# Graph layer with expert feed-forward: node rows kept as f32, added by VectorE, messages folded as f32

## What is computed

```python
def gnn(x, edge_attr, src, dst, ...):
    msg = relu(x[src] + edge_attr @ W_e + b_e)            # 21,250 x 512
    aggr = segment_sum(msg, dst, num_segments=N)          # 1,250 x 512
    h = (1.0 + eps) * x + aggr
    h = silu(batchnorm(h @ W1 + b1, g1, beta1))           # 1,250 x 1,024
    return silu(batchnorm(h @ W2 + b2, g2, beta2))
x = x + gnn(layernorm(x), ...)
x = x + ffn(layernorm(x), ...)    # each of 16 experts takes its 156 best tokens, gelu, weighted sum
```

## Time and profile before

| | us |
|---|---|
| median of 3 timed runs | 695.65 |
| their least and greatest | 694.82, 698.22 |
| span of the profiled execution | 727.8 |
| start, up to the first gather | 34.2 |
| edge loop, first gather to last fold | 34.2 to 329.1 |
| rest (dense layers, gate, experts) | 329.1 to 727.8 |

### The profile page before, as it was taken

One profiled execution on the slowest core, in us unless ns is written; L12 is line 12 of the kernel. 1 busy time (PEld: TensorE's weight loads), 2 busy tenths in 40 slices (PEclk: granted clock), 3 DMA queues, 4 the chain that ended last, 5 costly groups with the idle time before them and its releaser, 6 DMA issues.

```text
span 727.8 us, 14614 instructions
## 1 busy us (share of the span) xinstructions
PE 538.5 (74%) x5341; PEld 397.1 (55%) x5341; DVE 459.4 (63%) x1110; ACT 366.9 (50%) x630; POOL 358.3 (49%) x257
## 2 busy tenths in 40 slices
PE   2377788789868787798999985711599996888840
PEld 2244455446536454464555544511599986888830
DVE  7544456566746565576648867787679976668610
ACT  3843344445544454464648406630178875568720
POOL 1177777777777777600000000230347856688742
PEclk9998989999999999999999997755589999899985
DMA  7478786867777776804500034541269996643432
GB/s 189 144 192 208 189 205 180 208 179 202 200 190 198 191 198 180 199 19 166 181 1 1 1 115 141 174 158 41 58 202 281 265 268 181 180 101 54 69 40 35
DMA packets 75292, 108.91 MB, mean 150 GB/s; under 512 B 32139, under 2 KB 36803, under 8 KB 75246
## 3 DMA queue, kind: packets, MB, share of 16 engines
q0 software_dynamic: 43712, 53.95, 31.0%
q1 hardware_dynamic: 30364, 53.80, 24.6%
q10 hardware_dynamic: 1170, 0.55, 0.4%
HBM read 95.25 MB, written 12.79 MB: 148 GB/s over the span
## 4 chain that ended last, share of the span: by engine, by line
PE 46%; issue 16%; DMA 11%; DVE 9%; POOL 9%; ACT 6%; DVEq 1%; another core or an unknown queue 1%; ACTq 0%; POOLq 0%; SPq 0%
PE bank L1288 15%; PE bank L1269 9%; DMA out<-rows_z,idx 7%; PE bank L1247 5%; PE bank L1254 5%; POOL out L464 5%; PE bank L1256 4%; PE bank L1304 3%; POOL big L455 2%; PE bank L1230 2%; ACT big L576 2%; POOL big L445 1%; DVE edge_home L927 1%; DMA big<-token_rows,idx 1%; DMA pair<-node_rows,edge_home 1%
## 5 line engine op out<-in xcount | busy, mean ns | idle before, releaser
L918 DVE SCALAR_TENSOR_TENSOR big<-bank,big 125x512 f16<-125x512 f32 x170 | 116.4, 689 | 108.8 <-ACT big L576 63.6
L1288 PE MATMUL bank<-big,pair 128*128 128x156 f16 (+2 forms) x1824 | 173.6, 257 | 5.1 <-DVE big L1153 4.1
L576 ACT ACTIVATE big<-bank 125x512 f16<-125x512 f32 x170 | 98.8, 598 | 125.6 <-PE bank L1269 91.6
L1288 PEld LDWEIGHTS bank<-big,pair 128*128 128x128 f16 x1824 | 143.9, 102 | 30.4 <-DVE big L1153 6.3
L445 POOL DMA_INDIRECT big<-node_rows,edge_home x90 | 109.6, 1218 | 64.4 <-issue 54.2
L445 POOL DMA_INDIRECT pair<-node_rows,edge_home x80 | 98.2, 1227 | 30.0 <-issue 21.3
L464 POOL DMA_INDIRECT out<-rows_z,idx x32 | 85.1, 2658 | 45.4 <-DVE rows_z L1161 19.5
L1247 PEld LDWEIGHTS bank<-edge_home,big 125*128 125x128 f16 x1400 | 68.9, 99 | 55.9 <-issue 24.8
L475 POOL TENSOR_TENSOR big<-aggT,big 125x512 f16<-125x512 f32 x10 | 11.3, 1154 | 166.6 <-ACT big L663 166.6
L1247 PE MATMUL bank<-edge_home,big 125*128 125x64 f16 x1400 | 78.1, 195 | 15.4 <-issue 13.1
L455 POOL DMA_INDIRECT big<-token_rows,idx x32 | 51.1, 1596 | 52.6 <-DVE idx L1142 43.8
(11 more groups left out here) (207 smaller groups left out, 876.4 us busy)
## 6 DMA issues: line engine op xcount, KB each, us to landing
raw<-in_L_ffn_w SPq DMA_DIRECT2D x14, 1024.0 KB
edge_home<-in_L_ffn_w SPq DMA_DIRECT2D x6, 1024.0 KB
xs_home<-in_L_ffn_w SPq DMA_DIRECT2D x6, 1024.0 KB
aggT<-in_L_ffn_w SPq DMA_DIRECT2D x6, 1024.0 KB, 7.2
pair<-in_edge_attr SPq DMA_DIRECT2D x36, 140.0 KB
raw<-in_L_gnn_W SPq DMA_DIRECT2D x16, 256.0 KB
xs_home<-in_x SPq DMA_DIRECT2D x5, 448.0 KB
node_rows<-big SPq DMA_DIRECT2D x5, 448.0 KB
```

The lines of the kernel that those rows point to most:

```text
L576: act.activation(msg[:, b * J + j, 0, :], bank[j][0:P, :], ACT.Relu).then_inc(msg_hi, 1)
L918: dve.scalar_tensor_tensor(out=msg[:, b * J + j, 1, :], in0=bank[j][0:P, :], scalar=0.0, in1=msg[:, b * J + j, 0, :], op0=ALU.max, op1=ALU ...
L1288: last = pe.matmul(bk, weights(i, k), values(j, k), start=(begin and p == k == 0), stop=(end and p == 2 and k == n - 1), skip_group_check= ...
```

## The change

- `node_rows` holds each node as 512 f32 values, the normalised tile as it is; ScalarE's and VectorE's passes for the halves go. A node is still 2,048 B.
- VectorE adds the gathered row, times 8, to the product in bank j (L922 of the changed kernel) and writes the bank; the two row matmuls go, and with them VectorE's low half of the message. ScalarE writes the ReLU as one f32 message.
- The fold is four matmuls per j with f32 message and f32 one-hot instead of eight with f16.
- The bias comes in through two more rows, held at one, of a second copy of the transposed high features (`edge_hi_T`, 66 rows, one more ScalarE copy a step) against two more rows of `We_lo` (the bias in two parts). It stood in a 126th row of unit matrix and ring before.
- The parts in which landed rows are waited for are now j = 0 and 1, 2 and 3, 4. The credit to GpSimd comes from VectorE's addition.
- ScalarE's queue loads only the index lists, sources first; SyncE's the parameters: three arrays (four DMAs) around the first edge block, the stores of the table behind them, then the second edge block and the eight vectors and the gate.
- VectorE's list at the start is rewritten: sources' list first, statistics of the first group behind it, counting spread between the groups. The copies of transposed nodes to `aggT` go in turn to ScalarE (even tiles) and VectorE (odd ones). GpSimd clears half of the message buffer.

```diff
-        node_rows = nc.dram_tensor("node_rows", (N, 2 * H), F16).ap()
+        node_rows = nc.dram_tensor("node_rows", (N, H), F32).ap()
...
-            return (j + 1) // 2 - (j == 1)
+            return j // 2
...
-        rows = big[0:P + 1, 0:half].bitcast(F16).rearrange("p (s w h) -> p s w h", w=2, h=H)
-        late_rows = [pair16[i][0:P + 1].rearrange("p w a (s h) -> p (w a s) h", h=H)
-                     .rearrange("p (s w) h -> p s w h", w=2) for i in range(2)]
+        rows = big[0:P, 0:half].rearrange("p (s h) -> p s h", h=H)
+        late_rows = [pair16[i][0:P].rearrange("p w a h -> p (w a h)").bitcast(F32)
+                     .rearrange("p (s h) -> p s h", h=H) for i in range(2)]
...
-        msg = big[0:P, half:2 * half].bitcast(F16).rearrange("p (s w h) -> p s w h", w=2, h=H)
-        tabs = msg
+            return rows[:, r * J + j, :] if r < 2 else late_rows[r - 2][:, j, :]
+
+        msg = big[0:P, half:2 * half].rearrange("p (s h) -> p s h", h=H)
...
+            for half_rows in (slice(0, ED), slice(ED, 2 * ED)):
+                sp.dma_start(We32[half_rows, :], W_e).then_inc(params_in, 16)
             load_edges(0)
+            sp.dma_start(eps1[:], eps.partition_broadcast(128)).then_inc(params_in, 16)
+            sp.dma_start(be[:], b_e.partition_broadcast(2)).then_inc(params_in, 16)
+
+            for g in range(NT // XG):
+                sp.wait_ge(xn_ready, (g + 1) * XG)
+                for r0, r1 in SPRAY:
+                    sp.dma_start(by_tile(node_rows)[r0:r1, g * XG:(g + 1) * XG, :],
+                                 xn[r0:r1, g * XG:(g + 1) * XG, :]).then_inc(tab_out, 16)
             load_edges(1)
-
-            for g in range(NT // XG):
-                sp.wait_ge(tab_lo, (g + 1) * XG)
-                for r0, r1 in SPRAY:
...
-            sp.wait_ge(be_lo, 1)
-            for to in (rows, late_rows[0][:, 0:J], late_rows[1][:, 0:J]):
...
+            for v, k in ((b1, F1), (g1, F1), (beta1, F1), (b2, HK), (g2, HK), (beta2, HK)):
+                sp.dma_start(vecA[o:o + k, :], v.rearrange("(k p) -> k p", p=128)).then_inc(vec_in, 16)
+                o += k
...
+            sp.dma_start(gate_s[:], gate_t).then_inc(gate_in, 16)
...
+            pool.memset(msg[:, J:2 * J, :], 0.0).then_inc(hot_clear, 1)
...
-                        pool.indirect_dma_start(row(i % RING, j)[0:P].rearrange("p w h -> p (w h)"), None, node_rows,
+                        pool.indirect_dma_start(row(i % RING, j), None, node_rows,
                                                 bass.IndirectOffsetOnAxis(src_i[:, i, j:j + 1], 0)
                                                 ).then_inc(row_in[i % RING][part(j)], 16)
...
-            for to, ends_t, landed in ((ends[0], dst_t, dst_in), (ends[1], src_t, src_in)):
+            for to, ends_t, landed in ((ends[1], src_t, src_in), (ends[0], dst_t, dst_in)):
                 for r0, r1 in ((0, 32), (32, SB)):
                     act.dma_start(to[r0:r1], ends_t[r0:r1]).then_inc(landed, 16)
-            act.dma_start(We32[0:ED, :], W_e).then_inc(params_in, 16)
...
-                    act.wait_ge(xn_ready, t + 1)
-                    act.activation(tabs[:, t, 0, :], xn[:, t, :], ACT.Copy).then_inc(tab_hi, 1)
...
+            def edge_columns(b):
+
+                turned = bank[5][:].bitcast(F16)[:, 0:J * 128].rearrange("p (j c) -> p j c", j=J)
+                act.activation(edge_T[b][:, :, 0:P], turned[:, :, 0:P], ACT.Copy)
+                act.activation(edge_hi_T[b][0:ED, :, 0:P], turned[0:ED, :, 0:P], ACT.Copy).then_inc(edge_cp, 1)
+
...
-                        act.activation(edge_T[1 - b][:, :, 0:P], bank[5][:].bitcast(F16)[:, 0:J * 128]
-                                       .rearrange("p (j c) -> p j c", j=J)[:, :, 0:P],
-                                       ACT.Copy).then_inc(edge_cp, 1)
-                    act.wait_ge(msg_ps, CREDIT + n * J + j + 1)
+                        edge_columns(1 - b)
+                    act.wait_ge(row_used, CREDIT + n * J + j + 1)
                     act.wait_ge(folded, n * J + j + 1)
-                    act.activation(msg[:, b * J + j, 0, :], bank[j][0:P, :],
-                                   ACT.Relu).then_inc(msg_hi, 1)
-
-            act.wait_ge(tab_out, 16 * NT)
...
-            def table_lows(g):
-                for t in range(g * XG, (g + 1) * XG):
-                    dve.wait_ge(tab_hi, t + 1)
-                    dve.tensor_tensor(tabs[:, t, 1, :], xn[:, t, :], tabs[:, t, 0, :], ALU.subtract).then_inc(tab_lo, 1)
-
+            dve.wait_ge(src_in, 32)
+            dve.tensor_copy(ends_f[1], ends[1]).then_inc(ends_f_ready, 1)
+            statistics(0)
+            dve.wait_ge(dst_in, 32)
+            dve.tensor_copy(ends_f[0], ends[0]).then_inc(ends_f_ready, 1)
+            norm_terms(0)
+            dve.wait_ge(ends_ps, 1)
+            dve.tensor_copy(src_i[:], by_lane(bank[5])).then_inc(src_i_ready, 1)
+            statistics(1)
+            dve.wait_ge(ends_f_ready, 2)
+            dve.tensor_reduce(sb_base[:], ends_f[0], AX.X, ALU.min).then_inc(base_ready, 1)
+            norm_terms(1)
...
+            def edge_low(i):
+                dve.wait_ge(edge_hi, i + 1)
+                dve.tensor_tensor(edge_hl[i][:, :, 1, :], edge[i], edge_hl[i][:, :, 0, :],
+                                  ALU.subtract).then_inc(edge_lo, 1)
+
             dve.wait_ge(be_hi, 1)
-            dve.tensor_tensor(be16[:, 1, :], be[:], be16[:, 0, :], ALU.subtract).then_inc(be_lo, 1)
+            dve.scalar_tensor_tensor(out=We_lo[bias_rows, :], in0=be_high, scalar=be_low[bias_rows, 0:1], in1=be_scaled,
+                                     op0=ALU.mult, op1=ALU.add).then_inc(We_ready, 1)
+            dve.wait_ge(We_hi_ready, 1)
+            dve.scalar_tensor_tensor(out=We_lo[0:ED, :], in0=We32[0:ED, :], scalar=E_SCALE, in1=We_hi[0:ED, :],
+                                     op0=ALU.mult, op1=ALU.subtract).then_inc(We_ready, 1)
+            node_columns(1)
+            edge_low(0)
...
+                r = place % 2 * 2 + b
                 for j in range(J):
-                    dve.wait_ge(msg_hi, n * J + j + 1)
-                    dve.scalar_tensor_tensor(out=msg[:, b * J + j, 1, :],
-                                             in0=bank[j][0:P, :], scalar=0.0,
-                                             in1=msg[:, b * J + j, 0, :], op0=ALU.max,
-                                             op1=ALU.subtract).then_inc(msg_lo, 1)
+                    dve.wait_ge(edge_ps, n * J + j + 1)
+                    dve.wait_ge(row_in[r][part(j)], rows_landed(w, g, r, place, j))
+                    dve.scalar_tensor_tensor(out=bank[j][0:P, :], in0=row(r, j), scalar=E_SCALE,
+                                             in1=bank[j][0:P, :], op0=ALU.mult, op1=ALU.add).then_inc(row_used, 1)
...
-                for p in range(2):
-                    for k in range(HK):
-                        last = pe.matmul(bank[6 + b][:, k * WIN:(k + 1) * WIN],
-                                         msg[:, b * J + j, p, k * 128:(k + 1) * 128], onehot[b][:, j, :],
-                                         start=(j == p == k == 0), stop=(j == J - 1 and p == 1 and k == HK - 1),
-                                         skip_group_check=True)
+                for k in range(HK):
+                    last = pe.matmul(bank[6 + b][:, k * WIN:(k + 1) * WIN],
+                                     msg[:, b * J + j, k * 128:(k + 1) * 128], onehot[b][:, j, :],
+                                     start=(j == k == 0), stop=(j == J - 1 and k == HK - 1),
+                                     skip_group_check=True)
                 last.then_inc(folded, 1)
 
             def edge_product(j, b):
                 pe.matmul(bank[j][0:P, :], edge_T[b][:, j, 0:P], We_hi[:], start=True, stop=False,
                           skip_group_check=True)
-                return pe.matmul(bank[j][0:P, :], edge_T[b][:, j, 0:P], We_lo[:], start=False, stop=False,
-                                 skip_group_check=True)
+                pe.matmul(bank[j][0:P, :], edge_hi_T[b][:, j, 0:P], We_lo[0:ED + 2, :], start=False, stop=True,
+                          skip_group_check=True).then_inc(edge_ps, 1)
 
             def step(w, g, b, place):
 
                 n = w * SB + (g * 2 + b)
-                r = place % 2 * 2 + b
                 pe.wait_ge(edge_cp, n + 1)
                 for j in range(J):
-                    pe.wait_ge(msg_lo, n * J + j + 1)
+                    pe.wait_ge(msg_ready, n * J + j + 1)
                     edge_product(j, b)
-                    pe.wait_ge(row_in[r][part(j)], rows_landed(w, g, r, place, j))
-                    for p in range(2):
-                        last = pe.matmul(bank[j][0:P, :], ident_scaled[0:P + 1, 0:P], row(r, j)[:, p, :],
-                                         start=False, stop=(p == 1), skip_group_check=True)
-                    last.then_inc(msg_ps, 1)
```

(10 more changed lines are left out.)

174 lines of the change are left out of this document (76 added, 98 removed).

## The result

The changed kernel takes 876.0 us (median of 4 timed runs, 870.9 to 881.6) against 696.9 us for the kernel before; the ratio is 1.253 (95% interval 1.242 to 1.263). It was forecast at 690.5, with a range of 675 to 703: wrong, and by 185 us. The executions of most kernels here fall into two groups one or two per cent apart; a ratio compares the quicker group of both kernels, so it need not be the quotient of the medians beside it.

A forecast was written before the change was run, and what follows sets the result against it. The prediction took GpSimd's gather issue, 7.6 us a step, to bound the timed loop, with TensorE's 6.7 hidden: 695.65 - 8.1 (start) + 3.0 (tail) = 690.5 us; range for 8 in 10: 675 to 703.

The forecast's parts named there:

- TensorE's step: Edge loop, five j with their transposes: 6.7 us instead of 5.9, hidden under GpSimd's 7.6 with 0.9 us to spare.
- Rival 2: Edge loop: TensorE becomes the bound through its clock, a step 13.4 us at 1.2 GHz; 718 us in all, chance 0.15.
- TensorE busier than before: Argument against the slower-clock case, beside the granted clock of 0.99 from 160 us on.
- Its own formula: Loop with share f of time cold: 6.7/(1 - f/2) us a step, passing 7.6 at f = 0.24.
- If the unnamed pauses belong to the recording: TensorE's 0.2 to 0.5 us stops in the loop: absent from timed runs, whose loop ends some 28 us earlier, GpSimd-bound.
- rival 1: Edge loop: pauses are in timed runs too, TensorE binds and could come down to GpSimd's 7.6; 678 us, chance 0.17.
- The start: Up to the first gather: issued at 26.1 us against 34.24, 8.1 us earlier (7 to 9).
- The fold: TensorE per j: four f32 matmuls, two weight loads each, 0.86 us, 0.63 more than now.
- VectorE's addition: VectorE's pass per j, now writing PSUM: 0.7 us, bounds 0.6 and 0.9.
- ScalarE's second copy: ScalarE, one more copy a step: 0.70 us, its step 5.1 us, under 7.6.
- The tail: Last five folds after the last message: 6 us taken, bounds 4.3 to 8.6; tail grows by 3.0 us (1.3 to 5.6).

## Why the prediction was wrong

- **The step that failed is the clock.** The sum took TensorE's step at 6.7 us and called it hidden under 7.6. At full clock that is right, 6.66 us. At half clock it is 12.8, and the loop spent all of its 435 us there. Rival 2 named it, with a cold step of 13.4 us, but took the share of half clock from the worst stretch of before, 0.4, and spoke against itself with "TensorE busier than before". Its own formula with a share of one gives 34 x (13.4 - 7.6) - 5 = +192, 888 us. Measured 876.
- **Why the reason against it was false.** Busy time was taken for what brings the clock up. The changed TensorE was busy 100% of 442 us at 0.50; the kernel before 79 to 80% at up to 0.99. The change replaced two matmuls of 126 rows and 512 columns and a quick fold with short f32 streams behind long loads, and cut the second product to 66 rows. Two of these lifted the clock when that one alone was otherwise: the fold in f16 or with its operands exchanged, and 128 rows in the second product. With the row matmuls gone it took both, the short f32 fold and the 66 rows, to hold it down. The third, the row matmuls gone, was never tried alone: the kernel that had them beside an f32 fold had 128 rows in the second product too, and that suffices without them. Why rows and short streams count is not shown.
- **What paces the loop of before.** "If the unnamed pauses belong to the recording" doesn't hold on the second chip: a profiled execution as short as the timed ones has them. There rival 1's premise is right. With the clock in order the gathers take 260 to 262 us instead of 271, as it said in part; its gain of 17.5 us in all showed in no ratio, the best being 0.986, some 10 us.
- **The start**: 6.9 us earlier (27.36 against 34.24) where 8.1 was forecast, 7 to 9: just outside. The statistics end as worked out (18.11, forecast 18.3); the last normalising pass ends at 20.53, not 19.8, and the rest is the way from there to the gather. In the other traces of this start it was 26.5 to 27.0.
- **The fold**: 0.84 us a group at full clock (200.99 less 200.15 on the kernel with 66 rows and 512 added columns, lines below), forecast 0.86, and 1.60 at half. Two weight loads per matmul, not four (1,400 on the line, of 700 matmuls). Right.
- **VectorE's addition** into the bank: 0.70 us, forecast 0.7. ScalarE's second copy 0.69, forecast 0.70. Neither bound anything.
- **The tail**: the last five folds take 8.8 us (472.84 to 481.64), a little over the bounds of 4.3 to 8.6; 6 was taken. With 128 rows and 512 added columns, and the clock at 1.00 there, they took 4.67.

A fold at full clock, in the timeline of the kernel with 512 added columns:

```profile
199.93 0.38 PE L1274 MATMUL bank<-edge_home 128*125 128x256 f16 x2
200.15 1.00 PE L1252 MATMUL bank<-edge_home,big 125*128 125x64 f32 x8
200.99 0.38 PE L1259 MATMUL bank<-edge_home 128*125 128x512 f16 x1
201.21 0.38 PE L1261 MATMUL bank<-edge_home 66*125 66x512 f16 x1
```

## What to carry to other kernels

This is one kernel's lesson. When a change takes matmuls away from TensorE or makes them thinner, in rows or in columns per weight load, price every step at half clock too and say which of the two bounds holds; the slack against the next engine must cover the cold price, for the clock may not come back. Look for it by the granted clock of a stretch, since busy time is 100% either way, and try first what costs no time here: a full 128 rows where fewer are needed.

## What the runs showed of the hardware

- The changed kernel's stream of matmuls, without a gap, stayed at 1.2 GHz for 442 us. The Trainium skill ("TensorE: Matmul & The Clock Gate", Part 1) has the clock rise once TensorE has been busy; this trace doesn't agree, busy by the profile isn't enough.
- 62 rows more in one matmul of each group, against zero weights, took the loop from 0.50 to a clock between 0.65 and 0.99 as means of stretches of 60 us; 30 rows more (96) did nothing.
- With 512 columns added to the 66-row stream, the same kernel on the same chip took 719 us and 959.
- TensorE came to full clock in the start while it did nothing but f32 transposes (from 25.5 to 32.9 us). Their durations show it, 415 ns each up to 29 us and 270 from 30.4. The column of the granted clock doesn't: it reads 1.00 from 0 us on in these traces, with TensorE idle too, up to the first fall.

```profile
L1212 PE MATMUL bank<-ident,rows_z x16: 415/415/443, 25.5 to 29.0; 125*128 125x125 f32 x16
...
L1212 PE MATMUL bank<-ident,rows_z x11: 270/270/297, 30.4 to 32.2; 125*128 125x125 f32 x11
```
